# A four-layer network on one core: results stored as rows of channels from the last addition, layer statistics earlier in two layers, and unread matrix products in two convolutions

## What is computed

```
x = x + L0_conv(_ln_c(x))      # nearest of 1024 codes
t = t + L0_ffn(_ln_t(t))       # 8 experts, the two best per token, gelu
x = x + L1_conv(_ln_c(x))      # attention within neighbourhoods, 8 heads
t = t + L1_ffn(_ln_t(t))       # 8 experts, hidden size 64
x = x + L2_conv(_ln_c(x))      # squared cosine of all pairs of places
t = t + L2_ffn(_ln_t(t))       # 16 gated experts
x = x + L3_conv(_ln_c(x))      # cosines, batch normalisation
t = t + L3_ffn(_ln_t(t))       # 8 experts, gelu
```

## Time and profile before

| what | us |
|---|---|
| median of three runs | 958.12 |
| the profiled execution, its own time | 961.36 |
| span of its trace, first to last instruction | 959.5 |
| busy in the span: PE | 816.7 |
| DVE, ACT, POOL | 497.1, 404.8, 422.8 |

### The profile page before, as it was taken

One profiled execution on the slowest core, in us unless ns is written; L12 is line 12 of the kernel. 1 busy time (PEld: TensorE's weight loads), 2 busy tenths in 40 slices (PEclk: granted clock), 3 DMA queues, 4 the chain that ended last, 5 costly groups with the idle time before them and its releaser, 6 DMA issues.

```text
span 959.5 us, 16206 instructions
## 1 busy us (share of the span) xinstructions
PE 816.7 (85%) x5443; PEld 388.9 (41%) x5443; DVE 497.1 (52%) x1800; ACT 404.8 (42%) x750; POOL 422.8 (44%) x549
## 2 busy tenths in 40 slices
PE   5777698958898998877787899899999998899894
PEld 2323222215566666552224784333333226542221
DVE  5998855424345455554624543537464444434552
ACT  2001166623445455435343433434343334646662
POOL 2677366352333333324437824343735451114542
PEclk9999899975779799987778957999999999959997
DMA  9510133210000000003340004132323300011531
GB/s 183 94 31 10 30 96 118 85 41 1 2 1 2 2 2 2 2 2 111 113 133 2 1 0 124 49 109 79 83 79 85 92 18 2 1 40 56 144 107 56
DMA packets 48692, 52.54 MB, mean 55 GB/s; under 512 B 18832, under 2 KB 27172, under 8 KB 48612
## 3 DMA queue, kind: packets, MB, share of 16 engines
q1 hardware_dynamic: 47588, 50.46, 19.5%
q0 software_dynamic: 1024, 1.05, 0.6%
HBM read 49.78 MB, written 1.70 MB: 54 GB/s over the span
## 4 chain that ended last, share of the span: by engine, by line
PE 61%; DVE 13%; POOL 10%; issue 8%; ACT 5%; DMA 1%; POOLq 1%; SPq 0%; DVEq 0%; ACTq 0%
PE ps L683 18%; PE ps L688 12%; PE ps L1185 6%; DVE best L398 3%; DVE code L401 2%; PE ps L1230 2%; PE ps L1157 2%; PE ps L1180 2%; POOL work L1059 2%; PE ps L625 2%; PE ps L1556 2%; PE ps L1576 2%; DVE work L921 1%; PE ps L1774 1%; ACT work L802 1%
## 5 line engine op out<-in xcount | busy, mean ns | idle before, releaser
L683 PE MATMUL ps<-xT,wall 64*128 64x512 f32 x576 | 169.8, 672 | 5.7 <-ACT work L802 2.2
L688 PE MATMUL ps<-work,down 128*64 128x512 f32 x576 | 164.4, 652 | 6.7 <-POOL work L1047 6.1
L802 ACT ACTIVATE work<-ps,b1t 128x512 f32<-128x512 f32 x160 | 100.4, 685 | 79.6 <-PE ps L683 79.5
L921 DVE TENSOR_TENSOR work<-aq,ps 128x512 f32<-128x512 f32 x128 | 82.2, 684 | 97.3 <-PE ps L683 92.7
L1040 POOL TENSOR_TENSOR work<-xT,cwb 128x512 f32<-128x512 f32 x64 | 81.4, 1274 | 104.2 <-PE ps L683 78.8
L797 ACT ACTIVATE aq<-ps 128x512 f32<-128x512 f32 x128 | 69.4, 595 | 119.0 <-PE ps L683 118.9
L1059 POOL TENSOR_TENSOR work<-work 128x512 f32<-128x512 f32 x56 | 71.0, 1269 | 74.8 <-DVE work L947 72.1
L683 PEld LDWEIGHTS ps<-xT,wall 64*128 64x128 f32 x576 | 53.6, 203 | 110.6 <-issue 104.1
L947 DVE SCALAR_TENSOR_TENSOR work<-ps,b1t,cwb 128x512 f32<-128x512 f32 x64 | 47.9, 748 | 74.1 <-PE ps L688 56.9
L683 PE MATMUL ps<-work,wall 64*128 64x512 f32 x256 | 73.5, 651 | 9.9 <-DVE work L921 5.3
L289 PE MATMUL ps<-mt,xf 128*128 128x512 f32 x128 | 65.2, 635 | 17.0 <-DVE code L401 16.2
(11 more groups left out here) (228 smaller groups left out, 1397.4 us busy)
## 6 DMA issues: line engine op xcount, KB each, us to landing
cwb<-weight_rows SPq DMA_DIRECT2D x320, 128.0 KB, 3.1
wall<-in_L_ffn_w_dram SPq DMA_DIRECT2D x4, 512.0 KB
wall<-in_L_ffn_W_dram SPq DMA_DIRECT2D x4, 256.0 KB
out_dram<-tokens SPq DMA_DIRECT2D x8, 128.0 KB, 1.7
tokens<-in_x_dram SPq DMA_DIRECT2D x1, 896.0 KB, 6.1
ak<-in_L_conv_emb_dram SPq DMA_DIRECT2D x2, 256.0 KB, 3.7
zq<-in_L_conv_emb_dram,code POOLq DMA_INDIRECT x32, 2.5
down<-in_L_ffn_W_dram SPq DMA_DIRECT2D x2, 256.0 KB
```

What stands on the lines that cost most here:

```text
L683: ins = pe.matmul(m.ps[:, bank + half, :], m.wall[r, at + g * P:at + (g + 1) * P], x[r, :], start=True, stop=True)
L688: ins = pe.matmul(m.ps[half * C:half * C + C, bank, :], m.down[l][:, n % G, :], m.hid[:, n % 3, half, :], start=start, stop=True, skip_gro ...
L802: act.activation(m.hid[:, n % 3, half, :], m.ps[:, 2 * (n % 2) + half, :], ACT.Gelu, bias=bias)\
L921: dve.tensor_tensor(m.hid[:, n % 3, half, :], m.silu[:, n % 2, half, :], m.ps[:, 2 + half, :], ALU.mult)\
```

## The change

1. **Output.** In the last layer `back` is replaced by `lift`: PE multiplies the tokens of `X` by the identity, so that rows of channels lie in bank 6 of PSUM, in units 4, 14, 22 and 30. `add` then adds `acc`, whose rows are channels already, to that bank, and writes the sum to `y` (in the memory `tokens`). SP stores each super-block in two halves of 128 KB. The barrier and the four `out_` loops go, all but the stores.
2. **Statistics.** In layers 0 and 3 `stats`, `moments`, `scale`, `centre` and `norm` of the super-blocks 2 and 3 come two units earlier. `stats` gets a wait for DVE's own `moments` of the super-block before.
3. **Unread products.** `keep_warm` multiplies 224 columns of the weights by the identity into a part of a PSUM bank that nobody reads. Attention has 8 of them ahead of its slots, 3 behind `values` of the first four images, 1 in each `to_tokens` and 1 in each `outputs`; the third convolution has 6 ahead of its slots and 1 in each of the slots 3 to 9: 52 and 13.

```diff
-                  add=(13, 21, 29, None), stats=(None, None, 4, 12), moments=(None, None, 5, 13),
-                  scale=(None, None, 6, 14), centre=(None, None, 7, 15), norm=(None, None, 8, 16))
+                  add=(13, 21, 29, None), stats=(None, None, 2, 10), moments=(None, None, 3, 11),
+                  scale=(None, None, 4, 12), centre=(None, None, 5, 13), norm=(None, None, 6, 14))
...
-         exps=(None, 6, 11, 19), hits=(None, 6, 11, 19), combine=(None, 6, 12, 20)),
+         exps=(None, 6, 11, 19), hits=(None, 6, 11, 19), combine=(None, 6, 12, 20), back=(4, 14, 22, 30)),
 ]
+LAST = len(FFN) - 1
...
+    def lift(sb):
+
+        if sb:
+            pe.wait_ge(s.f_added, S0 + sb)
+        for t in range(TQ):
+            for half in range(2):
+                ins = pe.matmul(m.ps[half * C:half * C + C, 6, t * P:(t + 1) * P],
+                                m.X[:, sb * ST + half * TQ + t, :], m.ident[:], start=True, stop=True)
+        ins.then_inc(s.f_bps, 1)
...
-    back(SUPERS - 1, 7 if f["gated"] else 6)
+    if l < LAST:
+        back(SUPERS - 1, 7 if f["gated"] else 6)
...
     def stats(sb):
         if l == 0:
             dve.wait_ge(s.c0_added, 2 * sb + 2)
+        if S0 + sb:
+            dve.wait_ge(s.f_mv, S0 + sb)
...
     def add(sb):
+        if l == LAST:
+            dve.wait_ge(s.f_pw, p0 + (sb + 1) * (G - 1))
+            dve.wait_ge(s.f_bps, S0 + sb + 1)
+            dve.tensor_tensor(m.y[:, sb, :], m.acc[:, sb % 2, :], m.ps[:, 6, :], ALU.add).then_inc(s.f_added, 1)
+            return
...
+WARM = slice(288, 512)
+
+
+def keep_warm(pe, m, bank, n):
+
+    for _ in range(n):
+        pe.matmul(m.ps[:, bank, WARM], m.ident[:, :], m.wall[:, 0:WARM.stop - WARM.start], start=True, stop=True)
...
         ins.then_inc(s.c1_vp, 1)
+        if i < 4:
+            keep_warm(pe, m, 4, 3)
...
     def to_tokens(i):
         pe.wait_ge(s.c1_os, i + 1)
+        keep_warm(pe, m, 7, 1)
         pe.wait_ge(s.c1_xf, min(i + 6, IMAGES))
...
         ins.then_inc(s.c1_y, 1)
+        keep_warm(pe, m, 4, 1)
...
+    keep_warm(pe, m, 4, 8)
     c1_slots([(lambda i: by_query(i, 0), 2), (tokens, 3), (max_rows, 1), (to_tokens, -2),
...
     def also(j):
+        if 3 <= j <= 9:
+            keep_warm(pe, m, 7, 1)
...
+    keep_warm(pe, m, 7, 6)
     c2_slots([(tokens, 2), (dots, 1), (linear, 0), (outputs, -1)], also)
...
 def out_sync(sp, nc, m, s, out):
...
+    for sb in range(SUPERS):
+        sp.wait_ge(s.f_added, SUPERS * LAST + sb + 1)
+        for half in range(2):
+            at = sb * 4 + half * 2
+            sp.dma_start(out[at:at + 2].rearrange("i c h w -> c i (h w)"),
+                         m.y[half * C:half * C + C, sb, :].rearrange("c (i n) -> c i n", i=2)).then_inc(s.out_sent, 16)
+    sp.wait_ge(s.out_sent, 16 * 2 * SUPERS)
```

More of the change, by code:

```diff
@@ L673, in extras @@
                 weights(sb)
+            elif l == LAST:
+                lift(sb)
             elif f["gated"]:
@@ L1966, in prepare_act @@
     act.activation(m.b1t[:, :], m.ps[:, 7, 0:B1ROWS], ACT.Copy).then_inc(s.prepared, 1)
-def out_dve(dve, nc, m, s):
-    with dve.Fori(0, PAIRS) as g:
-        dve.wait_ge(s.out_t, g + 1)
-        x = m.X[:, bass.ds(g * PT, PT), :]
-        dve.tensor_copy(m.stage[:, :, :, :], x.rearrange("p (a i) c -> p i a c", i=2)).then_inc(s.out_x, 1)
-def out_pe(pe, nc, m, s):
-    pe.sem_inc(s.out_t, 1)
-    pe.sem_inc(s.out_y, 1)
-    with pe.Fori(0, PAIRS) as g:
-        pe.wait_ge(s.out_x, g + 1)
-        pe.wait_ge(s.out_y, g + 1)
-        for i in range(2):
-            ins = pe.transpose(m.ps[:, 0, i * P:(i + 1) * P], m.stage[:, i, :, :], m.ident[:])
-        ins.then_inc(s.out_t, 1)
-def out_act(act, nc, m, s):
-    with act.Fori(0, PAIRS) as g:
-        act.wait_ge(s.out_t, g + 2)
-        act.activation(m.y[:, bass.ds(g, 1), :].rearrange("p a n -> p (a n)"), m.ps[:, 0, 0:PLACES], ACT.Copy).then_inc(s.out_y, 1)
-def out_sync(sp, nc, m, s, out):
-    y = out.rearrange("(g a) c h w -> g (a c) (h w)", a=2)
-    with sp.Fori(0, PAIRS) as g:
-        sp.wait_ge(s.out_y, g + 2)
-        sp.dma_start(y[bass.ds(g, 1), :, :].rearrange("g p w -> p (g w)"),
-                     m.y[:, bass.ds(g, 1), :].rearrange("p a n -> p (a n)")).then_inc(s.out_sent, 16)
-    sp.wait_ge(s.out_sent, 16 * PAIRS)
+def out_sync(sp, nc, m, s, out):
+    for sb in range(SUPERS):
[5 more added lines that the diff above has]
+    sp.wait_ge(s.out_sent, 16 * 2 * SUPERS)
 FFN_SEMS = ["f_mv", "f_xn", "f_kept", "f_xps", "f_xt", "f_lps", "f_lg", "f_below", "f_ex", "f_cwd", "f_cps", "f_cwt", "f_cwo",
@@ L2011 @@
         "c0_scored", "c0_added", "ones_rows",
-        "weights_t", "tables", "padded", "prepared", "out_t", "out_x", "out_y", "out_sent", "part_done", "apart",
+        "weights_t", "tables", "padded", "prepared", "out_sent", "part_done", "apart",
         "dve_order", "pool_order"]
@@ L2097, in program @@
         m.normal = tokens[:, :].rearrange("p (t c) -> p t c", c=C + 1)
-        m.y = tokens[:, 0:TILES * C].rearrange("p (g n) -> p g n", g=PAIRS)
+        m.y = tokens[:, 0:TILES * C].rearrange("p (b n) -> p b n", b=SUPERS)
         m.xall = tokens[:, 0:TILES * C].rearrange("p (g n) -> p g n", g=PAIRS)
@@ L2152, in program @@
         m.cw = sb("cw", [P, ST * 16])
-        m.stage = sb("stage", [P, 2, 2, C])
         block = ctx.enter_context(nc.Block())
@@ L2179, in _ @@
             ffn_pe(pe, nc, m, s, 3)
-            barrier(pe, s, 7)
-            out_pe(pe, nc, m, s)
         @block.scalar
@@ L2198, in _ @@
             ffn_act(act, nc, m, s, 3)
-            barrier(act, s, 7)
-            out_act(act, nc, m, s)
         @block.vector
@@ L2218, in _ @@
             ffn_dve(dve, nc, m, s, 3)
-            barrier(dve, s, 7)
-            out_dve(dve, nc, m, s)
         @block.gpsimd
@@ L2238, in _ @@
             ffn_pool(pool, nc, m, s, 3)
-            barrier(pool, s, 7)
 SEEN = ([RANGES[0][:2]] * 4, [RANGES[1][:2]] * 3 + [RANGES[2][:2]])
```

## The result

The changed kernel takes 926.69 us (median of four runs, 924.27 to 928.85); the kernel before, beside it, 958.02 (948.33 to 965.3). The ratio is 0.9705 with a 95% interval of 0.9628 to 0.9782. Two later comparisons gave 0.9715 (0.9607 to 0.9823) and 0.9731 (0.9623 to 0.9838). Executions of one kernel differ here with the clock that is granted (the kernel before: from 944.72 us at a mean clock of 0.903 to 977.14 at 0.859); medians are over all executions, ratios leave out those more than 1.5% above the fastest of their kernel, which the kernel before has more often (8 of 11 in one comparison), so that every ratio is nearer to 1 than that of the medians.

The account below looks back on a forecast made before the run. PE at about half clock was taken to bound attention's start and the third convolution's second half. Terms -11.6 + 2.9 - 5.2 - 7.8 - 3.5 - 8.8 = -34.0 took 961.4 to 927.4, as median 924; range 910 to 933.

Parts of the forecast that it names:

- The end: From POOL's last sum to the last store: -11.6 us, or 9.3 saved if the two last stores run one behind the other.
- SP needs 0.31 to issue a transfer, once more for the second half: Kernel's end: the second half of the last store adds only another 0.31 us of issue by SP.
- The statistics: Layers 0 and 3: three waits for normalised tokens go (-7.7 us), later `combine` costs +2.5; together -5.2, bounds -10 and 0.
- each of the two layers pays 1.26: Layers 0 and 3: `stats` and `moments` ahead of `combine` delay PE's weight transposes by 1.74 - 0.48 = 1.26 us each.
- The price of a product: One unread product of 224 columns on PE takes 0.49 us at full clock and 0.91 at half.
- Attention, steady part: Attention's slots: products at both gaps prevent two slow slots, -8.4 + 0.6 = -7.8 us; bounds -8.4 and +16.
- Attention, start: Attention's first images: clock gives -12 us, eight products cost 6, twelve cost 2.5; sum -3.5, bounds -14 and +18.
- Third convolution: Seven slots at full clock give -15.4 us, six products cost 4.6, DVE's ranking 2; sum -8.8.
- the first rival: Third convolution: clock falls back in the slot with the router's transposes and stays down, +4.6 for -8.8; 937 us, chance 0.27.
- Attention stays slow: Attention: clock falls again at the start and in the steady part, two slow slots stay; 944 us, chance 0.13.
- Unread products on the path: Attention and third convolution: products delay PE and the clock returns nothing; up to 1003 us with all 65, chance 0.03.
- The statistics only move a wait: Layers 0 and 3: waits only change place, 0 for -5.2; 929 us, inside the forecast's range, no separate chance given.

Follow-up runs that it names:

- e8: Changed kernel without the six products ahead of the third convolution's slots, and with ACT's queue issuing the last store beside SP's: 936.4 us, ratio 0.9781.
- e4: Changed kernel with the statistics of super-blocks 2 and 3 back at units 4 and 12 in layers 0 and 3: 933.0 us, ratio 0.9687.
- e12: e10 with four more products in the third convolution, two ahead of the last image's products of places and two ahead of the last outputs: 926.2 us, ratio 0.9735.
- e7: Changed kernel without the 32 single products of attention's slots: 929.6 us, ratio 0.9713.
- e5: Changed kernel without the eight products ahead of attention's slots: 925.8 us, ratio 0.9664.
- e2: Changed kernel without attention's 52 products, the third convolution's 13 kept: 939.3 us, ratio 0.9801.
- e10: Changed kernel without attention's first eight products, with five ahead of the shares of each of the last two images and ACT's queue issuing the last store: 918.5 us, ratio 0.9595.
- e0: Changed kernel run again without an edit, beside e5, e6 and e7: 931.1 us, ratio 0.9715.
- e1: Changed kernel without any of the 65 unread products, output and statistics kept: 951.5 us, ratio 0.9952.
- e13: Changed kernel run again without an edit, beside e12: 925.7 us, ratio 0.9731.
- e3: Changed kernel without the third convolution's 13 products, attention's kept: 923.8 us, ratio 0.9616.
- e6: Changed kernel without the twelve products behind the values of attention's first four images: 926.9 us, ratio 0.9664.

## Why the prediction was right, and where not

The forecast was 924.0, measured 926.7; on the profiled execution 34.0 us were forecast and 32.5 came. The sum is better than its terms.

| term | forecast | profiled |
|---|---|---|
| end | -11.6 | -10.7 |
| layer 0: two waits, `cw` | -3.8 | -5.6 |
| layer 3: one wait, `cw`, lifts | +1.5 | -0.7 |
| attention, start to end | -11.3 | -3.0 |
| third convolution | -8.8 | -6.6 |
| not in the forecast: FFN 1, FFN 2, both other convolutions | 0 | -5.9 |

**The end** was right in mechanism; the step "SP needs 0.31 to issue a transfer, once more for the second half" was mis-sized. An issue is 0.61 here, and the two of them make 0.57 of the 0.86 that is missing. The Trainium skill, page "DMA: Bandwidth & Descriptors", section "Rules for kernel authors", would by its rule have had 9.3 for this part, as the prediction says; 10.7 came, and e8, with issues side by side, gained 0.2 of 0.6. So the trace agrees with it in part at most: the second half does not wait for a whole store of the first, and whether the two hinder each other is not shown.

**The lifts**: four of 0.93, from start to start, less three of 0.59 is 1.9 (forecast 2.9).

**The statistics** were right that the three waits go and that `cw` comes late, which is 1.49 in layer 0 (forecast 1.26; another wait there shrank by 0.35) and 2.07 in layer 3. What the sum left to its lower bound came: before, the clock fell behind the wait of 2.63, and the next two groups took 1.96 and 1.89 instead of 1.08 and 1.13:

```profile
168.36 1.96 PE L688 MATMUL ps<-work,down 128*64 128x512 f32 x4
170.25 1.89 PE L683 MATMUL ps<-xT,wall 64*128 64x512 f32 x4
```

e4 shows the stage's 5.7 by itself. In layer 3 the step "each of the two layers pays 1.26" was mis-sized: the wait of 2.63 became one of 2.07 and one of 0.37. From the first transposes of tokens to the last sum the stage is 1.1 longer (73.66 instead of 72.55), where the sum had 1.5. The -0.7 comes from the 1.8 us ahead of them, which no term held: in the stage's first 8 us the clock was 0.50 before, and 0.73 and then 1.00 after.

**The price of a product** was right. Ten records behind one another, five products, take 2.06 in e12, 0.41 each at full clock (forecast 0.49); at half clock, at the end of attention, one takes 0.90 (forecast 0.91). Single ones in the gaps of attention's slots leave them at 11.11.

**Attention, steady part.** The two slow slots went, as forecast. The steady middle gained 5.5 and not 7.8 because one slot still took 12.42 and the last two images a little longer. The reason that I gave, that a product at each gap keeps the clock up, fits the ten profiles that have them, none of which has a slot of 15.3, but is not all of it: e7 without them has one slow slot, not three.

**Attention, start: the step that failed.** I counted 20 products as 6.0 and 2.5 and 12 as the gain of the clock. The clock did rise, from 0.59 to 0.86, but the products keep PE busy 11.9 us in that stretch, and PE's busy time fell only from 42.5 to 41.1. Nearly all of what the clock gave went into the products, and the gain is 0.3. e5 shows that the eight of them needn't be there, and against e2 that the twelve alone gain 4.9. In the same step I left out the end of attention: the clock falls behind the wait of 2.9 for the shares, as it did before behind one of 3.4, the three singles there take 0.9 each, and 2.9 us are lost. e10 and e12 confirm it: with the wait filled, attention takes 4 us less than in e5.

**Third convolution.** The products held the clock past the router's transposes in each of the eleven profiles that have the seven singles (in e8 once it had risen), where it fell before. So the first rival was wrong. The sizes: the six take 4.66 (forecast 4.6), and the singles cost 0.27 in each of five slots, which I had put at nothing beside POOL. But PE comes to the outputs ahead of the router's transposes only 2.8 later than before (35.67 after the stage's start instead of 32.90), since before, too, the stage began at half clock (0.50 in the first 4 us of both). From there to the end e0, whose clock stays up, takes 23.6 instead of 36.7, 13.1 less; the sum had 15.4 less 2. In the profiled execution the clock fell at 553.59 behind a wait for DVE, which cost about 3.5 there (58.9 in e0), but FFN 2 was as much shorter. The Trainium skill's page "TensorE: Matmul & The Clock Gate", section "Part 4: PE-mode transpose", had spoken for that rival; no run here separates the transposes from the product beside them.

**The other rivals.** "Attention stays slow" is what e1 and e2 show without products, 229.3. "Unread products on the path" held for the start of attention alone. "The statistics only move a wait" is wrong for layer 0 by e4; for layer 3 nothing speaks against it.

**The part that was luck.** FFN 1 and FFN 2, which the change does not touch, are 6.1 shorter, most of the 8.3 by which attention fell short. In e1, without products, they are as long as before (80.1 and 212.5). FFN 2 is shortest in the three profiles whose clock fell late in the stage ahead of it (changed, e10 and e13: 210.1 to 210.3) and takes 211.5 to 214.4 in all others; what decides it is not shown. For FFN 1 see below.

## What to carry to other kernels

Unread products pay where one fall of the clock costs a whole slot and PE has gaps that hold them; put on the path at the start of a stage, they eat what the clock gives. Taking a wait away moves the start of the next stages, and where the clock falls there can move too, so count a gain only over the whole program: 6 us saved in layer 0 were gone in attention until the products were there. A step that is moved ahead on an engine can also put the wait behind another step of that engine, as in layer 3, where no gain is left. Compare stages of several profiles before a gain in one of them is called a gain, and look in the stage behind it for its return.

## What had not been expected

**FFN 1 takes 74.9 to 80.1 us with the same instructions.** Part of it goes with one pair of DVE's small products, `hit` times `prob` for super-block 2. In the kernel before (FFN 1 80.0), the pair for super-block 1 and that for super-block 2, and POOL's work beside the second:

```profile
447.07 0.36 DVE L885 TENSOR_TENSOR hit<-hit,prob 128x64 f32<-128x64 f32 x2
...
465.90 2.46 DVE L885 TENSOR_TENSOR hit<-hit,prob 128x64 f32<-128x64 f32 x2
```

```profile
465.79 2.48 POOL L1047 TENSOR_TENSOR work<-work,cwb 128x512 f32<-128x512 f32 x2
```

The pair that meets a free POOL takes 0.36. The one that meets POOL's two products ends 0.1 behind them, at 468.4. In e2 and e0 (79.9 and 79.0) it is 2.46 as well, in the changed kernel (76.4) 1.43, in e5 (74.9) 1.15. Over all profiles FFN 1 takes 77.6 to 80.1 in the six where the pair takes 2.46 and 74.9 to 77.0 in the eight where it takes less; but among these the order is lost, for e3, e6 and e13 have 0.36 and 75.8 to 76.1. The mean clock does not order them either: it is 0.78 before and 0.77 in the changed kernel. The Trainium skill, page "SBUF — State Buffer", section "SBUF: two separate sides", says that VectorE with two inputs in SBUF and GpSimd hold a common pair of ports one at a time, for a whole instruction; the trace agrees. These 1 to 2.1 us are less than FFN 1's difference of up to 5.2; what makes the rest was not tried.

**The spread.** The kernel before ranges over 32 us in one comparison (944.72 to 977.14, eleven executions), the changed one over 8 beside it (922.15 to 930.01, six), e3 and e12 over 24 and 20. Why one execution of the same program falls where another doesn't is not settled.
